# Inverse column transform of an AFNO block: real and imaginary parts of one row frequency stacked on the partitions, moved there by four GpSimd subtractions

## What is computed

```python
xf = jnp.fft.rfft2(x, axes=(1, 2), norm='ortho')            # after a layer norm
xf = xf.reshape(B, H, W // 2 + 1, NUM_BLOCKS, bs)
xr, xi = (jnp.real(xf), jnp.imag(xf))
o1r = relu(xr @ w1[0] - xi @ w1[1] + b1[0]);  o1i = relu(xi @ w1[0] + xr @ w1[1] + b1[1])
o2r = softshrink(o1r @ w2[0] - o1i @ w2[1] + b2[0], LAM)
o2i = softshrink(o1i @ w2[0] + o1r @ w2[1] + b2[1], LAM)
y = jnp.fft.irfft2(o2r + 1j * o2i, s=(H, W), axes=(1, 2), norm='ortho')
h = y + x + residual
return gelu(layer_norm(h) @ mw1 + mb1) @ mw2 + mb2 + h
```

## Time and profile before

| what | value |
|---|---|
| runs shown | 1069.82, 1069.26, 1067.75 us; median 1069.26 |
| span of the profiled execution | 1067.7 us (its own time, outside the span too, is not listed; the median lies 1.56 us above the span) |
| PE busy, weight load busy | 949.2 us (89%), 817.9 us (77%) |
| DVE, ACT, POOL busy | 719.9 (67%), 558.1 (52%), 272.1 us (25%) |
| granted TensorE clock, mean | 0.931 of full speed |
| PE matmuls of line 962 | 102.1 us busy |
| POOL subtractions of line 382 | 77.2 us busy, 64 instructions |

### The profile page before, as it was taken

The page is one execution under the profiler, slowest core; times in us unless marked ns, Lnnn a source line. Parts: engine busy times, 40 slices in busy tenths (PEclk is TensorE's granted clock), DMA queues, the critical chain, the costliest instruction groups (busy, mean ns, idle before and its releaser), DMA issues.

```text
span 1067.7 us, 18451 instructions
## 1 busy us (share of the span) xinstructions
PE 949.2 (89%) x6263; PEld 817.9 (77%) x6263; DVE 719.9 (67%) x2061; ACT 558.1 (52%) x1139; POOL 272.1 (25%) x107
## 2 busy tenths in 40 slices
PE   6989963887999999999999999999998999799787
PEld 6976553685689768976897689768976998499465
DVE  4456786189767776777676767676886688543762
ACT  0002011763776577657765776577647753775333
POOL 2000004034422332233223322332233224230110
PEclk8985565988999999999999999999999999989889
DMA  9922002011000300030003000200000000000001
GB/s 270 261 67 61 1 0 61 1 34 28 1 19 18 83 5 17 17 85 2 17 17 84 3 17 17 87 1 17 17 27 1 19 27 19 0 27 18 18 26 36
DMA packets 9956, 40.78 MB, mean 38 GB/s; under 512 B 1232, under 2 KB 1232, under 8 KB 8208
## 3 DMA queue, kind: packets, MB, share of 16 engines
q1 hardware_dynamic: 9888, 40.00, 13.4%
HBM read 27.15 MB, written 12.85 MB: 37 GB/s over the span
## 4 chain that ended last, share of the span: by engine, by line
PE 57%; DVE 16%; ACT 14%; issue 8%; DMA 4%; DVEq 0%; SPq 0%; ACTq 0%
PE psum L1024 13%; PE psum L909 9%; PE psum L1009 7%; PE psum L962 7%; ACT p_y L1112 7%; ACT o_g L1121 4%; PE psum L943 4%; PE psum L983 4%; PE psum L897 3%; PE psum L836 3%; DMA n<-x_dram 2%; DVE o_g L285 2%; PE psum L884 2%; DVE hbuf L568 2%; DVE stats L527 2%
## 5 line engine op out<-in xcount | busy, mean ns | idle before, releaser
L1153 ACT ACTIVATE hid<-psum,hbias 128x448 f32<-128x448 f32 x224 | 136.2, 634 | 132.2 <-PE psum L1009 131.5
L1024 PEld LDWEIGHTS psum<-prm,hid 128*112 128x112 f32 x1792 | 187.1, 182 | 8.5 <-ACT hid L1153 4.6
L1024 PE MATMUL psum<-prm,hid 128*112 128x96 f32 x1792 | 191.3, 267 | 2.3 <-ACT hid L1153 2.3
L354 POOL TENSOR_TENSOR hbuf<-hbuf,prm 112x1792 f32<-112x1792 f32 x15 | 63.3, 4217 | 328.4 <-DVE hbuf L595 328.4
L644 DVE TENSOR_TENSOR n2T<-psum,n2T 64x448 fp32r<-64x448 f32 x112 | 69.7, 622 | 102.5 <-ACT n2T L1145 101.3
L382 POOL TENSOR_TENSOR p_y<-over,under 116x512 f32<-116x512 f32 x64 | 77.2, 1208 | 201.7 <-ACT under L1171 201.6
L1009 PE MATMUL psum<-n2T,mw1h 128*128 128x448 f32 x224 | 101.8, 455 | 26.4 <-DVE n2T L644 12.8
L909 PEld LDWEIGHTS psum<-cst,hbuf 112*112 112x112 f32 x512 | 99.8, 286 | 20.5 <-issue 19.6
L909 PE MATMUL psum<-cst,hbuf 112*112 112x116 f32 x512 | 99.4, 358 | 18.1 <-DVE hbuf L777 18.1
L962 PE MATMUL psum<-cst,p_y 116*128 116x224 f32 (+1 forms) x480 | 102.1, 356 | 3.0 <-POOL p_y L382 3.0
L1100 ACT COPY u_r<-psum 112x464 f32<-112x464 f32 x64 | 35.0, 547 | 119.8 <-PE psum L909 119.8
(11 more groups left out here) (115 smaller groups left out, 1713.1 us busy)
## 6 DMA issues: line engine op xcount, KB each, us to landing
xin<-x_dram SPq DMA_DIRECT2D x9, 1568.0 KB, 8.9
out_dram<-oslice SPq DMA_DIRECT2D x56, 224.0 KB, 2.2
ybuf<-x_dram SPq DMA_DIRECT2D x2, 1568.0 KB, 18.9
fbuf<-x_dram SPq DMA_DIRECT2D x2, 1568.0 KB, 22.4
n<-x_dram SPq DMA_DIRECT2D x2, 1568.0 KB, 25.5
xin<-x_dram SPq DMA_DIRECT2D x4, 392.0 KB, 5.3
prm<-params_dram SPq DMA_DIRECT2D x1, 771.5 KB, 26.3
cst<-consts_dram SPq DMA_DIRECT2D x1, 652.0 KB, 18.9
```

What stands on the lines that cost most here:

```text
L354: nc.gpsimd.tensor_tensor(h, h, row("b1", WP), ALU.add).then_inc(h_ready, 1)
L1024: last = nc.tensor.matmul(t[0:ROWS, at:at + 96], hid[:, m, w % 2, (w // 2) * ROWS:(w // 2 + 1) * ROWS], pp("mw2")[:, 128 * m + zeros:128 * ...
L1153: nc.scalar.activation(hid[:, q % 2, q // 2, :], ring_c[k % RING_C][:, 0:4 * ROWS], ACT.Gelu, bias=hbias[:, q % 2:q % 2 + 1]).then_inc(c_a ...
```

## The change

One matmul's weights now hold one row frequency instead of two: its 58 rows of real parts on partitions 0 to 57 and its 58 rows of imaginary parts on partitions 64 to 121, so that real and imaginary parts are contracted in one pass. `inv_w` has 29 matmuls of 122 x 128 x 112 instead of 30 of 116 x 128 x 224. For this, `o_g` has blocks of 64 columns instead of 58, layer 2's outputs, `layer2`, `over` and `under` have 122 partitions (the second row frequency begins at partition 64), and GpSimd's one subtraction becomes four: (even row frequency, real part) stays on partitions 0 to 57, (odd, imaginary) stays on 64 to 121, (even, imaginary) goes from 0 to 57 to 64 to 121, and (odd, real) the other way. GpSimd waits for its own first two before the third, and for its fourth before it goes on. The table `invw` has 112 columns instead of 448, and `p_y` is set to zero once at the start.

```diff
-CONST_COLS = {"f1": 2 * KR, "f2": 4 * KF, "invw": 2 * 224, "invh": ROWS, "mask1": 128, "mask2": 128,
+CONST_COLS = {"f1": 2 * KR, "f2": 4 * KF, "invw": 112, "invh": ROWS, "mask1": 128, "mask2": 128,
...
+                nc.gpsimd.memset(p_y[:], 0.0).then_inc(s_ones, 1)
...
                         pool.wait_ge(shrunk, i * 8 + c + 1)
-                        yk = y_v[0:2 * KR, 4 * k:4 * k + L2_KP[k], :].rearrange("p k (m h j) -> p h k m j", h=2, j=CH)[:, half]
-                        a, b = (m[:, c % L2_BUFS, 0:n].rearrange("p (k m j) -> p k m j", m=4, j=CH) for m in (over, under))
-                        nc.gpsimd.tensor_tensor(yk, a, b, ALU.subtract).then_inc(y_ready, 1)
+                        a, b = (m[:, c % L2_BUFS, 0:n].rearrange("p (k r b j) -> p r k b j", r=2, b=2, j=CH) for m in (over, under))
+                        for n, (q, r) in enumerate(((0, 0), (1, 1), (0, 1), (1, 0))):
+                            if n == 2:
+                                pool.wait_ge(y_ready, i * 32 + 4 * c + 2)
+                            z = min(4 * k + L2_KP[k], (KF - q + 1) // 2)
+                            y = y_v[64 * r:64 * r + KR, 8 * k + q:2 * z - 1 + q:2, :].rearrange(
+                                "p k (b h j) -> p h k b j", b=2, h=2)[:, half]
+                            nc.gpsimd.tensor_tensor(y, a[64 * q:64 * q + KR, r, 0:z - 4 * k], b[64 * q:64 * q + KR, r, 0:z - 4 * k],
+                                                    ALU.subtract).then_inc(y_ready, 1)
+                        pool.wait_ge(y_ready, i * 32 + 4 * c + 4)
...
-                        for j in range(min(2, KHP - 2 * k)):
-                            kp = 2 * k + j
-                            n = min(2, KF - 2 * kp)
-                            for r in range(2):
-                                last = nc.tensor.matmul(t[:, j * 224:j * 224 + n * 112],
-                                                        y_v[0:n * KR, kp, 128 * r:128 * r + 128],
-                                                        inverse(r, n), start=(r == 0), stop=(r == 1))
+                        for j in range(min(4, KF - 4 * k)):
+                            last = nc.tensor.matmul(t[:, j * 112:j * 112 + 112], y_v[0:GR, 4 * k + j, :], cc("invw", GR),
+                                                    start=True, stop=True)
```

More of the change, by code:

```diff
@@ L180, in build @@
         oslice = sb("oslice", [ROWS, 2, SW * C])
-        layer2 = sb("layer2", [2 * KR, L2_BUFS, 512])
-        over = sb("over", [2 * KR, L2_BUFS, 512])
-        under = sb("under", [2 * KR, L2_BUFS, 512])
+        layer2 = sb("layer2", [GR, L2_BUFS, 512])
+        over = sb("over", [GR, L2_BUFS, 512])
+        under = sb("under", [GR, L2_BUFS, 512])
         neg_lam = sb("neg_lam", [128, 1])
@@ L940, in layer_2 @@
                     for j in range(L2_KP[k]):
[L942 to L944 removed]
+                        at = (half * KF + 2 * (4 * k + j)) * 64
+                        last = nc.tensor.matmul(t[0:GR, j * 128:j * 128 + 128], o_g[:, at:at + GR],
                                                 w2s[:, 128 * half:128 * half + 128], start=True, stop=True)
                     last.then_inc(pe_b, 1)
[L948 to L951 removed]
                 def inv_w(i, ks):
                     for k in ks:
[L956 removed]
+                        pe.wait_ge(y_ready, i * 32 + 4 * (4 + k // 2 + 1))
                         t = free_b(i, INVW + k)
[L958 to L964 removed]
+                        for j in range(min(4, KF - 4 * k)):
+                            last = nc.tensor.matmul(t[:, j * 112:j * 112 + 112], y_v[0:GR, 4 * k + j, :], cc("invw", GR),
+                                                    start=True, stop=True)
                         last.then_inc(pe_b, 1)
@@ L1167, in shrink @@
                     if c >= L2_BUFS or not isinstance(i, int) or i > 0:
-                        act.wait_ge(y_ready, i * 8 + c - L2_BUFS + 1)
-                    nc.scalar.activation(over[:, c % L2_BUFS, 0:n], v, ACT.Relu, bias=neg_lam[0:2 * KR, :])
-                    nc.scalar.activation(under[:, c % L2_BUFS, 0:n], v, ACT.Relu, bias=neg_lam[0:2 * KR, :],
+                        act.wait_ge(y_ready, i * 32 + 4 * (c - L2_BUFS + 1))
+                    nc.scalar.activation(over[:, c % L2_BUFS, 0:n], v, ACT.Relu, bias=neg_lam[0:GR, :])
+                    nc.scalar.activation(under[:, c % L2_BUFS, 0:n], v, ACT.Relu, bias=neg_lam[0:GR, :],
                                          scale=-1.0).then_inc(shrunk, 1)
@@ L1233 @@
 L2_BUFS = 2
-MEMSETS = 7
+MEMSETS = 8
 L1_PARTS = [(0, 15), (15, KF)]
@@ L1260, in constants @@
     wk = np.where((k == 0) | (k == KF - 1), 0.5, 1.0)
-    inv = np.zeros((2, 2, KF, 2, W, 2, 2))
-    for q in range(2):
-        for s, sign in enumerate((1.0, -1.0)):
-            inv[q, s, :, 0, :, q, 0] = (wk * cos).T
-            inv[q, s, :, 0, :, q, 1] = sign * (wk * sin).T
-            inv[q, s, :, 1, :, q, 0] = -(wk * sin).T
-            inv[q, s, :, 1, :, q, 1] = sign * (wk * cos).T
-    put("invw", inv.reshape(2 * KR, -1))
+    inv = np.zeros((GR, W, 2))
+    for s, sign in enumerate((1.0, -1.0)):
+        a, b = KF * s, KF * s + KF
+        inv[a:b, :, 0] = (wk * cos).T
+        inv[a:b, :, 1] = sign * (wk * sin).T
+        inv[64 + a:64 + b, :, 0] = -(wk * sin).T
+        inv[64 + a:64 + b, :, 1] = sign * (wk * cos).T
+    put("invw", inv)
     ih = np.zeros((2, 64, 2, H))
```

17 lines of the change are left out of this document (9 added, 8 removed).

## The result

| | changed kernel | kernel before, beside it |
|---|---|---|
| median of 4 runs each | 1093.44 us (1091.89 to 1095.98) | 1069.54 us (1067.75 to 1071.48) |
| span of the profiled execution | 1094.1 us | 1067.7 us |
| granted TensorE clock, mean | 0.918 | 0.931 |
| PE, DVE, POOL busy | 922.9, 752.7, 371.8 us | 949.2, 719.9, 272.1 us |

The account below looks back on a forecast made before the run. DVE, with GpSimd's bias in its path, was taken to bound the repeating pairs, not PE. Pair 0 +10, pairs 1 to 5 +12.3, pair 6 +5.2, pair 7 0, table -0.6: +26.9, 1096 us; range 1057 to 1112.

Parts of the forecast that it names:

- The price of a chunk: GpSimd's subtractions: four of 0.73 us, two waits and a register operation make 3.1 us; chunks come every 2.4 us.
- What bounds the pair: Pair 4: DVE's arrival sets the length through L595, L354, L568, without PE; a faster PE wins at most 1.45 us.
- A repeating pair: Pairs 1 to 5: GpSimd's backlog ends mean_rstd 3.9 us late, gaps take 1.45; each loses 2.45 us, the five 12.
- PE in slice 3: The shrink of c7 waits for c5, holding two gelus and PE back about 1 us, which shorter matmuls pay for.
- The Trainium skill's rule on ports: DVE beside GpSimd: one-input operations of mean_rstd would stand too, some 2 us more; left out of the sum.
- Pair 0: mean_rstd starts at 236.2 us, meets 5.4 us of GpSimd and ends at 245.1 instead of 235.06: +10 us.
- Pair 7: No mean_rstd in this place; PE's fourth MLP matmul 3.4 us late, six shorter groups give 3.4 back: 0.
- The table: Loads in the prologue: the table is 172 KB smaller at 270 GB/s, -0.6 us.
- The first: GpSimd's instructions cost half or run two at a time, nothing backs up: -9 to -12, 1058 us; chance 0.21.
- The second: DVE's short operations slip in between, GpSimd backs up but mean_rstd isn't held: +7, 1076 us; chance 0.09.
- The third: Moving across partitions, or GpSimd's wait on itself, is dear, 3.8 us a chunk: +60, 1130 us; chance 0.12.
- The fourth: The matmul gain is real where PE is the bound, all 38 us: 1031 us; chance 0.02.

Follow-up runs that it names:

- e2: Changed kernel without the two subtractions that move data and the wait between them (half of the spectrum left out): 1060.19 us, ratio 0.9939 to the kernel before.
- e7: The kernel of e2 with DVE's second-half ln1_subtract and ln1_rstd put ahead of the first half's ln1_gain: 1040.69 us, ratio 0.9758 to the kernel before.
- e4: Kernel before with spare GpSimd work behind c7, one tiny subtraction and five memsets, 3.6 us: 1072.00 us, ratio 1.0067.
- e1: Kernel before with only GpSimd's subtraction cut into four, all in place, with the same two waits: 1101.74 us, ratio 1.0349.
- e3: Kernel before with spare GpSimd work behind c7, six subtractions of constants, 4.25 us: 1076.37 us, ratio 1.0116.

## Why the prediction was right, step by step

Predicted were +26.9 us and 1096 us. The medians lie 23.9 us apart (1093.44), the profiled executions 26.4. The mechanism is the one that was told: a backlog of GpSimd, DVE's small operations standing beside it, and a path behind them without PE. That the sum came so close owes something to luck, since terms that were off cancelled.

- **The price of a chunk.** Predicted 4 x 0.73 and two waits, 3.1 us; measured 3.3. The instructions are exact (0.73), also the two that move data, and half of the partitions saves nothing. What was too small is the start of an instruction. I counted 0.07 us twice and nothing between instructions that don't wait. By the 3.13 us of a chunk, (3.13 - 0.73) / 3 = 0.80 us lie between the starts of any two of them, and the wait at the end costs 0.16. The text had allowed 0.3 us more for that.
- **Matmuls.** Predicted 0.112 us apart and 0.90 us for a group, measured 0.11 and 0.88. PE's busy time in `inv_w` went from 102.1 to 65.8 us.
- **What bounds the pair.** Predicted that a faster PE could win at most 1.45 us; e2 measured 1.2 at the end of that path and 0.6 for the pair, and e7 showed that the bound was L595, L354, L568 as said, since 3.3 us appear when it is opened. What PE's waiting does to its clock was not in the prediction. In the changed kernel it is small, 1.1 us in pair 3 and 0.2 in pairs 4 and 5.
- **A repeating pair.** Predicted +2.45 us, measured +2.6 to +2.8, and +3.7 once. Two of its terms were off and cancelled. `mean_rstd` started 1.1 us late (67.9 after the pair's start instead of 66.8), not 0.5. I had it held by c2, through the shrink of c4. The last to hold it was c3, through the shrink of c5, and at 3.3 us for a chunk c3 ended 0.5 later than I had it (60.1 after the pair's start, not 59.6). And it met GpSimd for 4.6 us, but took only 2.7 more, not 3.4: between two subtractions a waiting operation gets through, and early on the one behind it too. 1.1 + 2.7 = 3.8, predicted 3.9. Of these the gaps behind swallow 1.2, not 1.45, since 0.2 us of idle stay in the first of them.
- **PE in slice 3.** The shrink of c7 waited for c5 as said, but PE's fourth MLP matmul behind it came 2.0 us late (69.4 after the pair's start, before 67.3), not 1. DVE was later still, so the pair's length doesn't show it.
- **The Trainium skill's rule on ports.** By its page "SBUF — State Buffer", section "Who interferes with whom", operations with one input in a two-port mode would stand too. My sum left that out for want of a row. They do stand: L563 took 0.72 us instead of 0.20, and e4's L560 1.78. By that rule of the Trainium skill the sum was to be some 2 us higher than mine. It can't be told in the total, since the operations with two inputs stood less than I had them. The same section of the Trainium skill says that a DVE operation with two inputs doesn't clash with a GpSimd instruction that only writes; e4 shows it (0.26 us beside memsets).
- **Pair 0** +9.0 (predicted +10): `mean_rstd` from 236.86 to 244.35 (236.2 to 245.1). **Pair 6** +5.4 (predicted +5.2).
- **Pair 7**, predicted 0, measured -2.6. PE's fourth MLP matmul of slice 3 was late by 2.8 us, not 3.4, and what follows gave 3.8 back: -1.0 at the start of slice 5. The other 1.6 lie 30 to 60 us further on, where the change does nothing. One slice of the MLP took 5.87 us before and 4.92 after; the granted clock over it was 0.55 and 0.66. That is how the throttle happened to fall in two executions.
- **The table**, predicted -0.6, measured +0.3 for the prologue. The load of the constants is 484 KB instead of 652, but landed after 19.8 us instead of 18.9, so the smaller table brought no gain that shows. The prologue differs by up to 7 us between the profiled executions of these kernels (177.7 to 184.5 us to the first matmul of pair 0's `dft_h`), so this term can't be judged.
- **Rivals.** The first (half cost, or two at a time) fell: every subtraction starts 0.80 us after the one ahead. The rule of the Trainium skill's page "GPSIMD Engine Reference", section "Instruction dispatch", that a core may go on to the next instruction while others are busy, brought nothing, even for two that touch different halves (the first and second of a chunk). The second (small operations slip in) fell as a whole and was right in part, as told above. The third fell with e1: moving is free, and all that lies between and behind the four is 3.29 - 2.92 = 0.37 us a chunk. The fourth fell with e2.

Not tried: the changed kernel without GpSimd's waits on itself. The trace tells part of what they cost. The third subtraction, behind the first wait, starts 0.08 us after the second ends, like the second and the fourth, which have no wait. At a chunk's end 0.16 us stand idle, with the second wait, the wait for `shrunk` and a register operation in them, and how they share it isn't known. Nor is it known why plain rows of 256 elements without waits between (e3) start 0.70 us apart and the subtractions of a chunk 0.80, those of e2 too, which have no wait between the two.

## What to carry to other kernels

On GpSimd count instructions and elements of a partition, never partitions: cutting an operation in four by partitions and columns more than doubled its time (1.28 to 3.3 us with the waits), and moving data across partitions in it was free. Before work is taken off the engine with the highest busy share, find the stretch that sets the period; here a clash of DVE and GpSimd, and the clock that PE lost by standing for it, hid all but 0.6 of 4.7 us, and one line of DVE's order let 3.3 through, though by itself it is worth 0.2. Two changes that each look useless can be worth something only together: test a change to a busy engine also with the next bound opened.

## What was not expected of the hardware

- A memset of GpSimd lets DVE's operations with two inputs run at full speed (0.26 us) and stops one with one fp32 input in SBUF until all memsets queued behind each other are through (1.78 us instead of 0.20): it didn't get in between two of them. Between subtractions it did (L563 in the changed kernel, 0.72 us).
- GpSimd pays little for sharing with small operations of DVE: a chunk beside `mean_rstd` took 3.23 us instead of 3.13.
- Ahead of a full group of matmuls that write only 64 columns of the array, between full ones, the load engine stood 0.30 us. Inside a group they came 0.03 us apart on average (1.01 us for 32 loads), and their records start two at a time.
- PE that stands for 2.8 us in every pair can lose its clock there each time (e2, 0.50 from 664.4 to 667.8 us in pair 4), and part of what a shorter matmul wins is lost with it. In the changed kernel, which stands as long, the clock fell in some pairs and not in others.
